# Attention with four score banks, transposes in place, value strips and tokens two pairs ahead, on one core

## The chip, the cores and the metric

One Trainium2 chip, one core of it. The metric is the device time of one execution in microseconds, on that core. The kernel before was run three times: median 1459.58 us, 1443.99 to 1460.77.

## What is computed

An audio tower of two layers on x of shape (16, 256, 256), all in float32. Cut to what the change touches:

```python
# first layer, tokens: 16 x 256 rows of 256 -> 16 x 128 tokens of 256
xb = x.reshape(16, 128, 2, 256)
t = einsum('btki,oik->bto', xb, conv_w) + conv_b + xb.mean(axis=2)
h = layernorm(t) * gamma + beta
# first layer, attention on layernorm(h): 16 heads of 16, the last 64 positions; h + attn @ Wo.T
# first layer, experts: top 2 of 16 with capacity, and a shared gated product
# second layer, attention on layernorm(h): 16 heads of 16, causal; h + attn @ w_out
# second layer, experts: top 3 of 64, gelu, 128 slots each
```

In both layers a head's scores are a 128 x 128 matrix per batch: softmax(mask + q k / 4), times v, divided by the sum of the exponentials. A router on the normalised result chooses experts and slots for each token.

## The kernel before

The sixteen batches are worked in eight pairs. One core runs five queues, each written out by hand in order, with semaphores between them: SyncE issues loads, TensorE multiplies and transposes, ScalarE takes exponentials and copies banks out, VectorE takes maxima, norms and the routing, GpSimd takes the square roots, the affine part of the first norm and the scatters of rows to expert slots. The stages follow each other: attention of the first layer, half of the shared product, sixteen gated experts, the rest of the shared product, attention of the second layer, 64 dense experts. The change touches the two attention stages and the start.

The eight accumulation banks of 512 columns: two for scores, two for transposed probabilities, one for the mix (all sixteen heads of both batches), two front banks for the jobs that bring a pair in (transposed x, convolution, transposed normed tokens, q, k, v) and one back bank for the jobs that bring it out (inverse sums turned, spread over the columns, output product, feed-forward input turned, router, counts). Jobs of front and back take their bank in a fixed order, and each waits until the job before it in that bank has been copied out (`front`, `front_job`, `back_job`, L758 and L1061).

Scores of a batch come in four quarters b of four heads. `scores` (L817) multiplies 32 rows of q, at row group b, with the keys of two heads, twice per quarter. A product in float32 is two instructions. `greatest` (L1443, VectorE) adds the mask, moves the scores to `probs` and takes the maxima, `exponentials` (L1188, ScalarE) works on them in place, `turn_probs` (L827) transposes four heads into a turn bank, `keep_turned` (L1197, ScalarE) copies it to `probsT`, and `values` (L842) multiplies it with `v_wide`, in which each head's sixteen columns stand in a block of 128 otherwise zero, so that all heads add into the full mix bank. `step` alternates scores of batch s with transposes and products of batch a, the one before it: body i of the loop `skewed_loop` runs `step` for (scores of (i, 0), rest of (i-1, 1)) and then for (scores of (i, 1), rest of (i, 0)).

Between them stand the other parts: `turn_x` (L767) and `conv` (L776) for pair i+1, whose result `mix_tokens` (L1405, L1410) adds to half of the sum of x that GpSimd made in `sum_x` (L616); `project_qk` (L795), `project_v` (L803), `spread_inverse` (L877), `project_out` (L887), `turn_ffn_in` (L896), `route` (L903), `count` (L913). VectorE's part is `pairs` at the end of its block: `front_a` to `front_d` for the norms (statistics L1378 and L1383, application L1390), `normalise` (L1459), `residual` (L1465), `choose` for the experts (L1487 to L1519) with `weigh` (L1534 to L1541), and `place` for the slots (L1550 to L1565), whose first operation takes the counts out of the back bank.

SyncE loads x of pair 1 after the weights; then it fills the slot arrays with zeros (L479, 15 transfers, 13 of them of 1 MB) and then loads x of pairs 2 to 7, each behind the transposes of the pair before.

## Time and profile before

| what | us |
|---|---|
| median of three runs (lowest, highest) | 1459.58 (1443.99, 1460.77) |
| profiled execution, its span | 1452.52, 1450.8 |
| TensorE busy, VectorE, ScalarE, GpSimd | 1314.3, 532.5, 565.7, 360.2 |
| mean granted clock of TensorE | 0.943 |
| first attention stage, window 43 to 345 | 302 |
| second attention stage, window 637 to 911 | 274 |

The profile is of one execution. Busy time is per engine, and a matmul's end is modelled. The granted clock is a share of 2.4 GHz; it has two levels, 1.00 and 0.50. The idle time of an engine comes with what ended it.

### The profile page before, as it was taken

How to read it: one execution, taken by the hardware profiler on the slowest of the kernel's cores; microseconds unless marked ns; L12 is line 12 of the kernel's file. 1: busy time of each engine (PE TensorE's matmuls, PEld its weight loads, DVE VectorE, ACT ScalarE, POOL GpSimd, SP SyncE). 2: the span in 40 equal slices, each digit the busy share in tenths (PEclk: the TensorE clock that was granted, in tenths of full speed). 3: DMA queues.
4: the chain of work that ended last, by engine and by line, in shares of the span. 5: the costliest groups of instructions: out<-in, count | busy, mean ns of one | idle time of the engine just before them, and what ended most of it. 6: DMA issues, size and time to landing. Idle time of an engine off the chain costs nothing.

```text
span 1450.8 us, 25791 instructions
## 1 busy us (share of the span) xinstructions
PE 1314.3 (91%) x7680; PEld 1105.3 (76%) x7680; DVE 532.5 (37%) x2676; ACT 565.7 (39%) x1960; POOL 360.2 (25%) x343
## 2 busy tenths in 40 slices
PE   5899999986888898879999998199999999999996
PEld 4677777773577677547778777199999999999995
DVE  4356566542234443332555555212211221222121
ACT  1666666651122222135666665033223223322331
POOL 3123333212035444400122222312112212221221
PEclk8899999987999899999999999599999999999998
DMA  9700000001156556351000000269999999999993
GB/s 332 295 16 30 29 29 29 15 12 40 63 121 144 130 113 144 69 191 68 16 24 9 8 7 7 84 221 304 306 312 310 303 305 317 304 304 309 315 297 78
DMA packets 148816, 218.04 MB, mean 150 GB/s; under 512 B 9604, under 2 KB 117094, under 8 KB 148737
## 3 DMA queue, kind: packets, MB, share of 16 engines
q1 hardware_dynamic: 129824, 197.18, 40.1%
q0 software_dynamic: 18944, 20.28, 8.3%
q8 instruction: 23, 0.38, 0.1%
q14 instruction: 25, 0.20, 0.0%
HBM read 178.51 MB, written 45.19 MB: 154 GB/s over the span
## 4 chain that ended last, share of the span: by engine, by line
PE 75%; issue 6%; DVE 6%; ACT 4%; DMA 4%; POOL 3%; POOLq 0%; DVEq 0%; SPq 0%; ACTq 0%
PE bank L1104 16%; PE bank L1117 15%; PE bank L817 9%; PE bank L842 6%; PE bank L827 4%; PE bank L795 4%; PE bank L998 3%; PE bank L1044 3%; ACT probs L1188 2%; PE bank L887 2%; DMA stream<-arena,slot_token 2%; PE bank L776 2%; PE bank L1119 2%; PE bank L1008 2%; PE bank L803 1%
## 5 line engine op out<-in xcount | busy, mean ns | idle before, releaser
L1343 ACT ACTIVATE dhidT<-bank,b1T 128x128 f32<-128x128 f32 x512 | 145.9, 368 | 335.9 <-PE bank L1104 335.9
L1104 PE MATMUL bank<-probsT,arena 128*128 128x128 f32 x2048 | 241.4, 277 | 0.1
L1104 PEld LDWEIGHTS bank<-probsT,arena 128*128 128x128 f32 x2048 | 236.0, 193 | 0.5 <-DVE probsT L1751 0.5
L1117 PE MATMUL bank<-arena,dhidT 128*128 128x256 f32 x1024 | 231.6, 379 | 0.0
L1117 PEld LDWEIGHTS bank<-arena,dhidT 128*128 128x128 f32 x1024 | 189.8, 190 | 23.2
L1188 ACT ACTIVATE probs<-probs,neg_max 128x128 f32<-128x128 f32 x512 | 197.9, 390 | 10.4 <-DVE neg_max L1443 10.1
L720 POOL DMA_INDIRECT stream<-probsT,slot_token x64 | 98.9, 1545 | 402.9 <-DMA stream<-probsT,slot_token 352.8
L1772 DVE TENSOR_SCALAR probsT<-bank,slot_gate 128x256 f32<-128x256 f32 x64 | 30.9, 483 | 384.9 <-PE bank L1119 378.9
L1443 DVE CUSTOM_DVE_ANT_0 probs<-bank,mask 128x128 f32<-128x128 f32 x512 | 117.4, 286 | 124.9 <-PE bank L817 122.3
L817 PE MATMUL bank<-kT,qT 32*128 32x256 f32 x512 | 146.9, 412 | 4.5 <-DVE neg_max L1443 2.1
L634 POOL DMA_INDIRECT rows<-ffn_in,scatter_i x80 | 79.8, 998 | 259.4 <-DVE scatter_i L1565 207.2
L842 PE MATMUL bank<-probsT,v_wide 128*128 128x128 f32 x1024 | 141.4, 285 | 1.5 <-ACT probsT L1197 1.3
L1197 ACT ACTIVATE probsT<-bank 128x512 f32<-128x512 f32 x128 | 75.2, 589 | 157.3 <-PE bank L827 117.4
L842 PEld LDWEIGHTS bank<-probsT,v_wide 128*128 128x128 f32 x1024 | 130.2, 199 | 2.2 <-ACT probsT L1197 2.1
L817 PEld LDWEIGHTS bank<-kT,qT 32*128 32x128 f32 x512 | 86.8, 191 | 39.0 <-issue 20.8
L1188 ACT ACTIVATION_READ_ACCUMULATOR probs<-probs,neg_max 128x1 f32 x512 | 97.1, 190 | 0.0
L691 POOL DMA_INDIRECT stream<-arena,slot_token x48 | 72.9, 1518 | 57.2 <-DVE arena L1714 45.3
L827 PEld LDWEIGHTS bank<-ident,probs 128*128 128x128 f32 x512 | 55.7, 145 | 41.1 <-issue 36.1
L827 PE MATMUL bank<-ident,probs 128*128 128x128 f32 x512 | 86.3, 293 | 0.0
L1056 PE MATMUL bank<-arena 128*128 128x256 f32 (+3 forms) x288 | 70.8, 394 | 13.2 <-DVE arena L1714 13.1
L1319 ACT ACTIVATE arena<-bank 128x320 f32<-128x320 f32 (+1 forms) x48 | 20.9, 436 | 152.5 <-PE bank L1044 116.1
L1056 PEld LDWEIGHTS bank<-arena 128*128 128x128 f32 (+3 forms) x288 | 48.4, 175 | 29.9 <-DVE arena L1714 17.5
(172 smaller groups left out, 1719.8 us busy)
## 6 DMA issues: line engine op xcount, KB each, us to landing
arena<-L_ffn_w SPq DMA_DIRECT2D x128, 1024.0 KB, 7.4
rows<-zeros SPq DMA_DIRECT2D x13, 1024.0 KB, 13.1
drows<-rows SPq DMA_DIRECT2D x64, 132.0 KB, 7.7
arena<-L_ffn_w_gate SPq DMA_DIRECT2D x16, 352.0 KB
arena<-L_ffn_w_up SPq DMA_DIRECT2D x16, 352.0 KB
early<-rows SPq DMA_DIRECT2D x16, 264.0 KB, 2.7
early<-x SPq DMA_DIRECT2D x8, 512.0 KB
arena<-L_ffn_w_down SPq DMA_DIRECT2D x16, 256.0 KB
```

Of the source, the lines that this page charges most:

```text
L634: g.indirect_dma_start(L.rows, bass.IndirectOffsetOnAxis(ap=scatter_i[:, k, t:t + 1], axis=0), ffn_in[:, t, :], None, bounds_check=L.E * L ...
L720: g.indirect_dma_start(stream, bass.IndirectOffsetOnAxis(ap=slot_token[:, u, 0:1], axis=0), dy[:, u % 2, :], None, bounds_check=N + NCT * ...
L817: last = pe.matmul(score_bank[b % 2][:, 2 * m * P:2 * (m + 1) * P], qT[row:row + 32, m, t, :], kT[row:row + 32, m, t, :, :], start=True, s ...
L827: last = pe.transpose(turn_bank[b % 2][:, j * P:(j + 1) * P], probs[:, t, head(b, j), :], ident[:, :])
L842: last = pe.matmul(mix_bank[:, col:col + P], v_wide[:, DC * t + m, own * P:(own + 1) * P], probsT[:, b, j * P:(j + 1) * P], start=b == 0 a ...
L1056: mm = pe.matmul(bank[6 + (NCT * u + s) % 2][0:m, 0:D], hidT[u][0:fm, j, r:r + m], down_w[u][0:fm, j, :], start=j == 0, stop=j == NFT - 1)
L1104: mm = pe.matmul(bank[2 + 2 * (u % 2) + half][:, jj * P:(jj + 1) * P], w1_sb[u][:, c, j * P:(j + 1) * P], drowsT[:, u % 2, c, :], start=c ...
L1117: pe.matmul(bank[6 + u % 2][:, 0:D], dhidT[:, u % 2, j, :], w2_sb[u][:, j, :], start=j == 0, stop=False)
L1188: last = act.activation(probs[:, t, hd, :], probs[:, t, hd, :], ACT.Exp, scale=-1.0, bias=neg_max[:, t, hd:hd + 1], accum_out=exp_sum[:, t ...
L1197: act.activation(probsT[:, b, :], turn_bank[b % 2][:, :], ACT.Copy).then_inc(L.turned, 1)
L1343: last_ = act.activation(dhidT[:, u % 2, j, :], bank[2 + 2 * (u % 2) + half][:, jj * P:(jj + 1) * P], ACT.Gelu, bias=b1T[:, j, bass.ds(e, 1)])
L1443: last = dve.tensor_tensor_reduce(probs[:, t, hd, :], score_bank[b % 2][:, j * P:(j + 1) * P], L.mask[:, :], -1.0, 3e38, ALU.add, ALU.min, ...
```

## The change

- Four score banks instead of two, and no turn banks. `scores` writes all sixteen heads of a batch in eight products, the four row groups in turn, with one signal at the end; it waits for all four copies of the batch before. `turn_probs` writes over the scores in their own bank.
- The copies of three quarters stay on ScalarE (`keep_turned`); the last is a copy on VectorE (`keep_last_turned`).
- `v_wide` becomes `v_pad`: two heads to a strip of 32 columns. `values` writes strip b of the mix bank, four strips in turn, a whole batch at a time.
- Tokens two pairs ahead: `turn_x` and `conv` of pair i+2 run in body i, pair 1 ahead of the loop. x of pair 1 is loaded before the router's inputs, x of pairs 2 and 3 behind the zero fills.
- The half sum of x goes into the diagonal of the convolution weights, once; `sum_x` goes.
- The order of all queues in `pairs` is new; each body finishes its own transposes. Job numbers of the banks come from two lists of the order.

```diff
-        score_bank, turn_bank, mix_bank = bank[0:2], bank[2:4], bank[4]
+        score_bank, mix_bank = bank[0:4], bank[4]
...
-        HALF = (P // HD) * (P + HD)
-        v_wide = sb("v_wide", [P, 2 * DC, HALF])
+        STRIP = 2 * HD
+        v_pad = sb("v_pad", [P, 2 * DC, (P // HD) * STRIP])
...
+            order = [(0, INVERSE)]
+            for i in range(1, PAIRS + 2):
+                for p, k in ((i - 2, COUNT), (i - 1, SPREAD), (i - 1, OUT), (i - 1, TURN_FFN), (i - 1, ROUTE), (i, INVERSE)):
+                    if 0 <= p < PAIRS:
+                        order += [(p, k)]
+            return {job: n for n, job in enumerate(order)}
...
-            load_x(1, False)
             sp.wait_ge(const_p, 3)
             fill_zeros()
-            with sp.Fori(2, PAIRS) as i:
+            for i in range(2, 4):
+                load_x(i, False)
+            with sp.Fori(4, PAIRS) as i:
...
+                wait(pe, L.turned, 6 * i + 3 * t)
+                wait(pe, L.turned_last, 2 * i + t)
                 for m in range(DC):
-                    last = pe.matmul(score_bank[b % 2][:, 2 * m * P:2 * (m + 1) * P], qT[row:row + 32, m, t, :],
-                                     kT[row:row + 32, m, t, :, :], start=True, stop=True)
+                    for b in range(SBANKS):
+                        row = 32 * b
+                        last = pe.matmul(score_bank[b][:, 2 * m * P:2 * (m + 1) * P], qT[row:row + 32, m, t, :],
+                                         kT[row:row + 32, m, t, :, :], start=True, stop=True)
...
-                n = 8 * i + 4 * t + b
-
-                wait(pe, L.exp_done, n + 1)
-                wait(pe, L.turned, n - 1)
+
+                wait(pe, L.exp_done, 8 * i + 4 * t + b + 1)
                 for j in range(HEADS_PER_BANK):
-                    last = pe.transpose(turn_bank[b % 2][:, j * P:(j + 1) * P], probs[:, t, head(b, j), :], ident[:, :])
+                    last = pe.transpose(score_bank[b][:, j * P:(j + 1) * P], probs[:, t, head(b, j), :], ident[:, :])
...
+                    m, r = divmod(j, 2)
                     col = (2 * m + t) * P
-                    last = pe.matmul(mix_bank[:, col:col + P], v_wide[:, DC * t + m, own * P:(own + 1) * P],
-                                     probsT[:, b, j * P:(j + 1) * P], start=b == 0 and j == 0,
-                                     stop=b == SBANKS - 1 and j % 2 == 1, skip_group_check=True)
+                    for b in range(SBANKS):
+                        own = 2 * b + r
+                        last = pe.matmul(mix_bank[b * STRIP:(b + 1) * STRIP, col:col + P],
+                                         v_pad[:, DC * t + m, own * STRIP:(own + 1) * STRIP], probsT[:, b, j * P:(j + 1) * P],
+                                         start=j == 0, stop=r == 1, skip_group_check=True)
...
+                    ahead = L is L0 and there(i + 2, PAIRS)
+                    if now:
+                        scores(L, i, 0)
                     if before_:
-                        turn_inverse(L, i - 1)
-                    if next_ and L is L0:
-                        turn_x(i + 1)
-                    if next_ and L is L1:
-                        turn_normed(L1, i + 1)
+                        values(L, i - 1, 1)
+                    if there(i - 2, PAIRS):
+                        count(L, i - 2)
                     if before_:
                         spread_inverse(L, i - 1)
-                    if next_ and L is L0:
-                        conv(i + 1)
-                    if next_ and L is L1:
-                        project_qk(L1, i + 1, 0)
-                        project_qk(L1, i + 1, 1)
+                    if now:
+                        project_v(L, i)
+                        turn_probs(L, i, 0, 0)
+                    if ahead:
+                        turn_x(i + 2)
+                    if now:
+                        turn_probs(L, i, 0, 1)
                     if before_:
                         project_out(L, i - 1)
                     if now:
-                        step(L, (i, 1), (i, 0), beside_second)
-                    else:
-                        beside_second(SBANKS - 1)
-                    if next_ and L is L0:
-                        turn_normed(L0, i + 1)
+                        turn_probs(L, i, 0, 2)
+                        turn_probs(L, i, 0, 3)
+                        scores(L, i, 1)
+                        values(L, i, 0)
+                    if next_:
+                        turn_normed(L, i + 1)
+                    if now:
+                        turn_probs(L, i, 1, 0)
+                    if ahead:
+                        conv(i + 2)
+                    if next_:
+                        project_qk(L, i + 1, 0)
+                    if now:
+                        turn_probs(L, i, 1, 1)
+                    if next_:
+                        project_qk(L, i + 1, 1)
+                    if now:
+                        turn_probs(L, i, 1, 2)
                     if before_:
+                        turn_ffn_in(L, i - 1)
                         route(L, i - 1)
-                    if next_ and L is L0:
-                        project_qk(L0, i + 1, 0)
-                        project_qk(L0, i + 1, 1)
-                    if next_:
-                        project_v(L, i + 1)
+                    if now:
+                        turn_probs(L, i, 1, 3)
+                        turn_inverse(L, i)
...
+                    ahead = L is L0 and there(i + 2, PAIRS)
+                    if now:
+                        exponentials(L, i, 0, 0)
+                    if there(i - 2, PAIRS) and L is L1:
+                        router_exp(L1, i - 2)
                     if before_:
                         keep_spread(L, i - 1)
                     if now:
-                        step(L, (i, 1), (i, 0), beside_second)
-                    else:
-                        beside_second(SBANKS - 1)
-                    if next_ and L is L0:
-                        keep_normedT(L0, i + 1)
+                        exponentials(L, i, 0, 1)
+                        keep_turned(L, i, 0, 0)
+                        keep_v(L, i)
+                        exponentials(L, i, 0, 2)
+                        keep_turned(L, i, 0, 1)
+                        exponentials(L, i, 0, 3)
+                        keep_turned(L, i, 0, 2)
+                    if ahead:
+                        keep_xT(i + 2)
+                    if now:
+                        exponentials(L, i, 1, 0)
+                    if next_:
+                        keep_normedT(L, i + 1)
+                    if now:
+                        exponentials(L, i, 1, 1)
+                        keep_turned(L, i, 1, 0)
+                        exponentials(L, i, 1, 2)
+                    if next_:
+                        keep_q(L, i + 1)
+                    if now:
+                        exponentials(L, i, 1, 3)
+                        keep_turned(L, i, 1, 1)
+                    if next_:
+                        keep_k(L, i + 1)
+                    if now:
+                        keep_turned(L, i, 1, 2)
+                    if before_:
+                        keep_ffn_inT(L, i - 1)
+                    if now:
+                        keep_inverse(L, i)
...
+            for k in range(2):
+                for c in range(DC):
+                    own = conv_wT[:, 2 * k + c, c * P:(c + 1) * P]
+                    last = dve.scalar_tensor_tensor(out=own, in0=ident[:, :], scalar=0.5, in1=own, op0=ALU.mult, op1=ALU.add)
+            last.then_inc(conv_ready, 1)
...
-                    dve.scalar_tensor_tensor(out=tok[:, t, :], in0=x_sum[:, t, :], scalar=0.5, in1=front_bank[b][:, 0:D],
-                                             op0=ALU.mult, op1=ALU.add).then_inc(L0.front_free[b], 1)
+                    dve.tensor_tensor(tok[:, t, :], front_bank[b][:, 0:D], conv_b[:, :], ALU.add).then_inc(L0.front_free[b], 1)
...
+            def keep_last_turned(L, i, t):
+
+                wait(dve, L.turn_full, 8 * i + 4 * t + SBANKS)
+                wait(dve, L.pv_done, 2 * i + t)
+                dve.tensor_copy(probsT[:, SBANKS - 1, :], score_bank[SBANKS - 1][:, :]).then_inc(L.turned_last, 1)
...
+                    ahead = L is L0 and there(i + 2, PAIRS)
                     if now:
-                        if before_:
-                            invert(L, i - 1, 1)
                         greatest(L, i, 0, 0)
                     if there(i - 2, PAIRS) and L is L1:
                         less_greatest(i - 2)
                     if now:
-                        greatest(L, i, 0, 1)
-                    if now and next_ and L is L1:
+                        for b in range(1, SBANKS):
+                            greatest(L, i, 0, b)
+                    if next_ and L is L0:
+                        front_c(i + 1)
+                    if next_ and L is L1:
                         front_a(L1, i + 1, False)
-                    if there(i - 2, PAIRS) and L is L1:
-                        weigh(L1, i - 2)
-                    if not now and there(i - 2, PAIRS):
-                        place(L, i - 2)
-                    if not now and before_:
-                        invert(L, i - 1, 1)
-                    if now:
-                        greatest(L, i, 0, 2)
-                        greatest(L, i, 0, 3)
-                    if next_ and L is L1:
-                        front_d(L1, i + 1)
-                    if now and there(i - 2, PAIRS):
+                    if there(i - 2, PAIRS):
+                        if L is L1:
+                            weigh(L1, i - 2)
                         place(L, i - 2)
                     if before_:
                         normalise(L, i - 1)
-                    if next_ and L is L0:
-                        front_a(L0, i + 1, False)
-                    if before_:
                         residual(L, i - 1)
+                        residual_stats(L, i - 1)
+                    if next_:
+                        front_d(L, i + 1)
                     if now:
+                        keep_last_turned(L, i, 0)
                         invert(L, i, 0)
-                        greatest(L, i, 1, 0)
-                    if before_:
-                        residual_stats(L, i - 1)
-                    if next_ and L is L0:
-                        front_b(i + 1)
-                    if now:
-                        greatest(L, i, 1, 1)
-                        greatest(L, i, 1, 2)
+                        for b in range(SBANKS):
+                            greatest(L, i, 1, b)
                     if before_:
                         expert_input(L, i - 1)
-                    if next_ and L is L0:
-                        front_c(i + 1)
+                    if ahead:
+                        front_a(L0, i + 2, False)
+                        front_b(i + 2)
                     if now:
-                        greatest(L, i, 1, 3)
-                    if next_ and L is L0:
-                        front_d(L0, i + 1)
+                        invert(L, i, 1)
+                        keep_last_turned(L, i, 1)
                     if before_:
                         choose(L, i - 1)
-                    if before_ and L is L0:
-                        weigh(L0, i - 1)
-
-                skewed_loop(dve, PAIRS, 2, body)
+                        if L is L0:
+                            weigh(L0, i - 1)
```

GpSimd's order in the first layer becomes: scale for the norm of i+1, scatter of i-2, scale for the feed-forward norm of i-1, addition of the input, scale and affine part of the tokens of i+2. `count` and `spread_inverse` keep their products; `spread_inverse` and `route` wait in addition for the copy of the job that feeds them.

## Rows read from the trace of the kernel before

**Rows 1.** Windows: the two attention stages, and one pair of each

```profile
core 0: us, PE busy (x) PEld busy (x) DVE busy (x) ACT busy (x) POOL busy (x), PEclk, DMA share, GB/s
43.00:345.00 302.00, 278.83 (x1600) 223.40 (x1598) 161.89 (x935) 174.33 (x633) 83.91 (x100) 0.95 0.13 47
188.80:225.90 37.10, 35.45 (x212) 28.66 (x211) 22.10 (x125) 22.97 (x84) 11.81 (x15) 1.00 0.08 29
...
637.00:911.00 274.00, 258.61 (x1468) 206.02 (x1468) 137.70 (x860) 170.56 (x647) 53.41 (x69) 0.94 0.11 40
750.40:781.90 31.50, 31.00 (x186) 24.79 (x187) 18.32 (x113) 21.02 (x82) 7.80 (x10) 1.00 0.05 19
```

**Rows 2.** TensorE timeline, one first-layer pair (start us, us, engine, line, operation, tiles, count)

```profile
188.74 3.72 PE L776 MATMUL bank<-conv_wT,early 128*128 128x256 f32 x16
...
211.15 1.89 PE L803 MATMUL bank<-wT,normedT 128*128 128x256 f32 x8
212.97 1.12 PE L817 MATMUL bank<-kT,qT 32*128 32x256 f32 x4
214.03 0.66 PE L827 MATMUL bank<-ident,probs 128*128 128x128 f32 x4
...
216.16 1.06 PE L842 MATMUL bank<-probsT,v_wide 128*128 128x128 f32 x8
...
224.76 1.12 PE L877 MATMUL bank<-exp_invT,own_rows 16*128 16x256 f32 x4
```

**Rows 3.** Groups by line, the same pair (busy us, mean ns, idle before, releaser)

```profile
L1188 ACT ACTIVATE probs<-probs,neg_max 128x128 f32<-128x128 f32 x32 | 12.4, 391 | 0.4 <-DVE neg_max L1443 0.3
...
L1443 DVE CUSTOM_DVE_ANT_0 probs<-bank,mask 128x128 f32<-128x128 f32 x32 | 7.3, 284 | 5.7 <-PE bank L817 5.7
...
L1197 ACT ACTIVATE probsT<-bank 128x512 f32<-128x512 f32 x8 | 4.7, 587 | 9.2 <-PE bank L827 9.2
...
L1170 ACT ACTIVATE kT<-bank,parity 128x512 f32<-128x512 f32 x2 | 1.3, 684 | 1.1 <-PE bank L795 1.1
```

**Rows 4.** VectorE timeline, the same pair

```profile
194.93 0.69 DVE L1465 TENSOR_TENSOR h<-h,bank 128x512 f32 x1
...
201.89 0.74 DVE L1378 BATCH_NORM_STATS2 stats<-h 128x6 f32 x2
...
207.75 0.19 DVE L1487 TENSOR_TENSOR logits<-bank,rb 128x32 f32<-128x32 f32 x1 [1.62 <-PE bank L903]
...
211.89 0.16 DVE L1541 TENSOR_TENSOR weight<-top_v,rsmall 128x4 f32<-128x4 f32 x1
...
222.41 0.19 DVE L1550 COPY count_sb<-bank 128x32 f32<-128x32 f32 x1 [0.52 <-PE bank L914]
...
224.23 0.15 DVE L1565 TENSOR_TENSOR scatter_i<-slotf,tmpf 128x4 int32<-128x4 f32 x1
```

**Rows 5.** TensorE timeline, first scores of the second layer

```profile
642.87 1.14 PE L817 MATMUL bank<-kT,qT 32*128 32x256 f32 x8
```

**Rows 6.** Timelines of the SyncE queue and of GpSimd, start of the kernel

```profile
55.90 58.04 SPq L407 DMA_DIRECT2D early<-x  x3
...
67.57 1.28 POOL L616 TENSOR_TENSOR early<-early 128x512 f32<-128x512 f32 x1 [10.67 <-DMA early<-x]
```

**Rows 7.** Windows: three stretches at the end of the first attention stage

```profile
290.00:300.00 10.00, 7.99 (x55) 6.18 (x53) 4.02 (x29) 7.77 (x32) 1.33 (x2) 0.94 0.01 2
300.00:310.00 10.00, 9.76 (x25) 6.57 (x26) 3.77 (x23) 2.13 (x9) 3.60 (x5) 0.50 0.11 41
310.00:345.00 35.00, 23.59 (x139) 19.43 (x138) 13.53 (x82) 13.49 (x40) 7.48 (x8) 0.74 0.04 12
```

**Rows 8.** TensorE timeline: first scores of pairs 1 and 7, and of pair 7

```profile
65.07 1.13 PE L817 MATMUL bank<-kT,qT 32*128 32x256 f32 x4
...
286.25 1.12 PE L817 MATMUL bank<-kT,qT 32*128 32x256 f32 x4
...
868.40 1.10 PE L817 MATMUL bank<-kT,qT 32*128 32x256 f32 x4 [0.32 <-issue]
```

273 lines of the change are left out of this document (128 added, 145 removed).

## Prediction

> **What bounds the kernel now.** I read the page's chain of waits first: three quarters of the span are TensorE, and its lines change with the stage, so the question is which stages the change touches. The windows answer it: first-layer attention from 43 to 345 us and second-layer attention from 637 to 911 us, 576 of 1450.8 us [rows 1]. The gated experts, the shared product and the dense experts between and behind them keep their code; I take them at their time. Then I took one pair of each layer. A first-layer pair lasts 37.1 us with TensorE busy 35.45 of it at granted clock 1.00; a second-layer pair lasts 31.5 us at clock 1.00. ScalarE and VectorE have 22 to 23 us of work per pair [rows 1]. TensorE's queue is the bound, and the other two run beside it because one batch's scores alternate with the preceding batch's transposes and products. The steady pace over whole stages is (286.25 - 65.07)/6 = 36.9 us, and (868.40 - 642.87)/7 = 32.2 us in the second layer, whose first pair is shorter [rows 5, 8].
>
> **The change part by part, TensorE's work.** Scores of one quarter of a batch, four instructions, take 212.97 to 214.03 = 1.06 us; a batch has four, 4.2 us [rows 2]. Now all four row groups follow each other. The old trace has that in small: where the pipeline is empty two quarters stand back to back, and eight instructions take the 1.14 us that four take elsewhere [rows 5, 2]. Their pace, 1.14 less the tail of about 0.25, is 0.11 us each; sixteen make 1.8 us. Bounds: 4.2 us (no overlap) and 16 x 0.22/4 = 0.9 us (four at once, at the pace of the 16 instructions of 256 columns in 3.56 us). I take 1.8, the nearest row. Products with the values: a quarter is eight instructions in about 0.9 us, a batch 3.6 [rows 2]. As strips of 32 output partitions no row shows them; bounds 3.6 and 0.9 us, I take 1.9, since the score row halves too. The rest of a pair (transposes 0.5 a quarter, convolution 3.6, the query and key product 3.6, value and output products 1.8 each, spread 1.0) stays. TensorE's own work falls from 35.4 to about 27 us in the first layer.
>
> By the Trainium skill ("TensorE: Matmul & The Clock Gate", Packing small matmuls), four row tiles gave 3.07 times and three column tiles 2.38 times; estimated from that page, scores would be 1.4 and products 1.5 us, 0.8 us a batch below my sum. The trace agrees that row groups overlap.
>
> **What takes its place.** The transposes now overwrite the score banks, so scores of a batch wait until all four banks of the preceding one are copied out (three by ScalarE, one by VectorE). Batches no longer overlap, and the pace is that of a chain from copy to copy. I follow it through a first-layer pair in the new order of the queues; zero is the end of the last copy before it.
>
> First half. VectorE has the choice of experts queued behind that copy and ahead of the next maxima: 207.75 to 212.05 = 4.3 us [rows 4], and 0.4 because the exponential it needs is behind a copy on ScalarE: 4.7. Scores (1.8) are hidden under it, so neither packing nor banks helps here. Four maxima quarters at 0.85 (thirty-two heads, 7.3 us busy, [rows 3]): 8.1. Statistics of the next pair 0.74 + 0.25 + 0.1 [rows 4]: 9.2. Only then comes the copy of the counts, the first operation of the slot calculation, 0.2: 9.4. It matters because there is one back bank: the spread of the inverses may not begin before the counts have left it. Behind the spread TensorE holds the value product and the first transpose, and ScalarE holds the copy of the spread ahead of the second quarter's exponentials. So: spread 1.05, value product 1.8, transpose and its landing 0.8 [rows 2]: 13.1. ScalarE copies it and the values, 0.5 each: 14.1. The second early transpose of x waits for that bank: 0.6, next transpose 0.5, output product 1.8 and 0.25 to VectorE: 17.2. Residual 0.7, statistics 1.1, normalisation 0.7 [rows 4], then the new last copy 0.7 (512 columns from a bank, as the residual): 20.4. TensorE idles about 5 us ahead of the spread.
>
> Second half, from 0 again. Scores 1.8, products 1.9, transpose of the normed tokens 0.5, first transpose by 5.0 (its exponentials end at 4.5: scores 1.8, landing 0.25, maxima 0.9, exponentials 1.55, from 12.4 us for 32 heads [rows 3]), convolution two pairs ahead 3.6, query product 1.8, landing: 10.65. ScalarE, which holds that copy ahead of the last exponentials, goes on: 0.6, exponentials 1.55, copy 0.5, keys 1.25, copy 0.5, feed-forward input 0.6 [rows 3]: 15.65. Routing 0.85, last transpose and landing 0.8, last copy 0.7: 18.1. The pair: 38.5 us at full clock, against 37.1.
>
> Second layer: choice without weights 3.5, maxima and one small operation 3.5, statistics 1.1, weights 0.6, counts 0.3: 9.0; spread, value product, transpose 3.65; two copies 1.0; exponentials, copy, exponentials 3.6; last transpose and copy 1.5: 18.75. Second half, now bound by ScalarE because there is no convolution: 16.15. Together 34.9 at full clock against 31.5.
>
> **The clock.** Stretches in which TensorE was busy 8.0 of 10 us were followed by 10 us at 0.50, which is 1.2 GHz, and the 35 us with 23.6 us busy had 0.74 [rows 7], while the full pair had 1.00 [rows 1]. The new pair is busy 27 of 38.5 us, 70%, with a gap ahead of the spread in each. I take 0.87 as mean clock, between 0.74 and 1.00, so work in the chain grows by 15%: 17.5 us of the first-layer chain is TensorE (5.75 in the first half, 11.75 in the second), +2.6, pair 41.1; 7.0 us in the second layer, +1.1, pair 36.0.
>
> The same page (HAM oscillation) says that pauses between bursts send the array back to its half rate: a rule against this change. The trace agrees: [rows 7] show the drop behind a thinner stretch. By it alone, with every pair dipping, the time is that of the clock rival below.
>
> **The start.** The tokens of pair 2 are now transposed in pair 0, between its first and second probability transpose, but their load stays behind the zero fills in SyncE's queue: issued at 55.90, landed at 67.57, where GpSimd's sum was waiting for it [rows 6]. TensorE, strictly in order, waits there. From 67.5: two transposes 1.2, probability transpose 0.8, copy 0.5, exponentials 1.55, transpose 0.8, last copy 0.7: 73. Second half without routing 18: first scores of pair 1 at 91, before 65.07 [rows 8]. The loss is about 26 us; with the load early enough it would be some 2 us.
>
> **Smaller parts, taken at nothing.** The halved sum of x goes into the convolution weights (four small operations once, ahead of a VectorE fill that shrinks by three quarters): saves GpSimd 1.3 and VectorE 0.8 us a pair, both off the chain. Moving one load of x ahead of the router loads delays these by 2 to 3 us; the normalised first pair hides that. One more pair unrolled, no cost. GpSimd's scatters start after the slots, at 11 us, and land before the feed-forward input is due in the second half; if not, that is 1 to 3 us a pair. The stages' tails stay as they are: the last copies no longer straddle pairs, but the slots come later; between -6 and +3 us each.
>
> **The sum.** First layer: 91, pair 1 at 33.5 (no choice, no slots yet), five at 41.1: first scores of pair 7 at 330, against 286.25: +44. Second layer from its first scores: 28, 29.5, five at 36.0: 237.5 against 868.40 - 642.87 = 225.5: +12. The profiled execution took 1452.52 us (span 1450.8 and 1.7 around it): 1452.5 + 56 = 1508. It is 7 us below the median of the three runs shown, 1459.58, within their spread.
>
> **Rivals.**
> 1. Clock near 0.70 in both stages. For: the 0.74 of [rows 7]. Against: TensorE works through most of the second half. Pairs 38.5 + 17.5 x 0.43 = 46 and 37.9: ten pairs add 34 us, 1542.
> 2. Full packing and full clock: scores 0.9, products 1.0. Pairs 36.8 and 34.2, start still late: first layer +19, second +2, 1474. For: the row of eight. Against: the gap per pair.
> 3. The other side: VectorE's small operations do not stand in the chain, neither the choice ahead of the maxima nor the counts ahead of the spread (the choice over while the last exponentials run). Pairs 30.6 and 30.4; with the late start -12 and -15: 1426. Against it stands the order of VectorE's queue and the single back bank; for it, that VectorE is busy only 22 of 37 us. It decides once a first-layer pair lasts less than about 31 us, or 33 with a start that is not late.
> 4. The packing does not come: scores 4.2, products 3.6, about 4.1 and 3.5 us a pair more: 1554. [Rows 5] speak against it for scores; if only the strips fail, 1524, inside my range.
>
> **Chances.** Forecast 0.52 (own range 1480 to 1530), rival 1 0.12, rival 2 0.20, rival 3 0.12, rival 4 0.04. A measurement of this kernel can tell about 2%, 29 us. Slower by over that: most of the forecast, rivals 1 and 4: 0.63; within: the rest of the forecast and rival 2: 0.25; faster: 0.12. The range reaches from 1455, most of rival 2, to 1542.
>
> **What would show it.** Right: a TensorE gap of some 20 us that a load of x ends, between 45 and 68 us; first-layer pairs 39 to 43 us apart; sixteen score instructions in about 2 us; the spread starting within 0.1 us of the copy of the counts; maxima starting where the choice ends, not where the scores end; PEclk under 0.95 in both stages. Wrong: pairs under 36 us, ScalarE waiting for the spread less than 1 us, or no wait on x.

## The result, and the profile after

The changed kernel takes 1521.52 us (median of 4 runs, 1518.83 to 1525.41) against 1458.17 us for the kernel before: a ratio of 1.045, interval 1.041 to 1.049. It is slower. The profiled execution took 1520.47 us, with a span of 1518.7 against 1450.8 before. Line numbers from here on are those of the changed kernel: scores L862, probability transposes L870, values L886, spread L908, output product L918, maxima L1484, last copy L1493, counts copy L1597. In an experiment's rows some lie a few lines further on.

The windows come first. A pair has two halves, each from the first scores of a batch to those of the next. The first row is one pair's length of the first layer, from second scores to second scores; the second row is the first half in it, the third the second half behind it. The fourth is a second-layer pair, the last the thin part of a first half. They answer to [rows 1].

```profile
core 0: us, PE busy (x) PEld busy (x) DVE busy (x) ACT busy (x) POOL busy (x), PEclk, DMA share, GB/s
183.25:224.20 40.95, 28.75 (x211) 22.21 (x211) 20.74 (x126) 21.28 (x82) 10.75 (x13) 0.79 0.08 26
201.15:224.20 23.05, 15.01 (x97) 11.12 (x97) 12.52 (x78) 10.73 (x42) 6.02 (x8) 0.67 0.14 46
224.20:242.10 17.90, 13.74 (x114) 11.09 (x115) 8.22 (x48) 10.54 (x41) 4.73 (x5) 0.95 0.00 0
818.84:856.32 37.48, 26.57 (x186) 19.82 (x187) 19.22 (x117) 19.75 (x80) 7.85 (x10) 0.73 0.03 9
205.30:216.50 11.20, 6.24 (x19) 4.53 (x17) 6.62 (x49) 3.78 (x17) 3.83 (x5) 0.50 0.07 24
```

TensorE is busy for less time, 28.75 us instead of 35.45 in a pair, yet the pair lasts 40.95 us instead of 37.10. No engine is full any more: the pace is that of a chain. Now TensorE's timeline of that pair (start us, us, engine, line, operation, tiles, count, idle before and releaser):

```profile
201.15 2.14 PE L862 MATMUL bank<-kT,qT 32*128 32x256 f32 x16 [0.16 <-issue]
203.22 1.94 PE L886 MATMUL bank<-probsT,v_pad 128*32 128x128 f32 x32
...
210.32 2.07 PE L908 MATMUL bank<-exp_invT,own_rows 16*128 16x256 f32 x4 [4.96 <-DVE count_sb L1597]
212.32 3.78 PE L845 MATMUL bank<-wT,normedT 128*128 128x256 f32 x8
...
224.20 1.15 PE L862 MATMUL bank<-kT,qT 32*128 32x256 f32 x16 [2.06 <-DVE probsT L1493]
225.27 1.08 PE L886 MATMUL bank<-probsT,v_pad 128*32 128x128 f32 x32
```

The packing works. At full clock sixteen score products take 1.15 us, where four quarters of 1.06 took 4.2 [rows 2]; thirty-two strips take 1.08 us, where values took 3.6. But at 201.15 they run at half rate, then TensorE stands still for 4.96 us, and the spread and the value product behind it take 2.07 and 3.78 us instead of 1.12 and 1.89: 2.84 us from the clock alone. VectorE's timeline says what TensorE waited for:

```profile
199.54 0.69 DVE L1493 COPY probsT<-bank 128x512 f32<-128x512 f32 x1 [4.02 <-PE bank L870]
200.15 0.18 DVE L1534 TENSOR_TENSOR logits<-bank,rb 128x32 f32<-128x32 f32 x1
...
204.76 0.16 DVE L1588 TENSOR_TENSOR weight<-top_v,rsmall 128x4 f32<-128x4 f32 x1
205.68 0.29 DVE L1484 CUSTOM_DVE_ANT_0 probs<-bank,mask 128x128 f32<-128x128 f32 x1 [0.76 <-DVE weight L1588]
...
209.07 0.75 DVE L1423 BATCH_NORM_STATS2 stats<-h 128x6 f32 x2
209.92 0.25 DVE L1428 BATCH_NORM_AGGREGATE moments<-stats 128x2 f32<-128x6 f32 x2
210.08 0.18 DVE L1597 COPY count_sb<-bank 128x32 f32<-128x32 f32 x1
```

The choice of experts runs from 200.15 to 204.92, the maxima start behind it, 0.76 us later, although the scores were there at 203.3, then come the statistics, and only at 210.08 do the counts leave the back bank. The spread starts at 210.32. At the start, TensorE's wait for the tokens of pair 2, and the DMA queue of SyncE that explains it:

```profile
64.89 1.97 PE L806 MATMUL bank<-ident,early 128*128 128x128 f32 x8 [22.91 <-DMA early<-x]
```

```profile
19.14 34.70 SPq L526 DMA_DIRECT2D rows<-zeros  x15
...
55.22 1.27 SPq L452 DMA_DIRECT2D early<-x  x1
```

The page's groups show the sums over the whole kernel (busy us, mean ns, idle before and releaser): 52.4 us of waiting for the counts, and 119.7 us in which ScalarE's exponentials wait for maxima. The last row is that group in the window 183.25 to 224.20 alone: 8.2 us, against 0.3 in the pair before [rows 3].

```profile
L1228 ACT ACTIVATE probs<-probs,neg_max 128x128 f32<-128x128 f32 x512 | 198.2, 392 | 119.7 <-DVE neg_max L1484 119.7
...
L862 PE MATMUL bank<-kT,qT 32*128 32x256 f32 x512 | 53.3, 545 | 24.9 <-DVE probsT L1493 19.6
L908 PE MATMUL bank<-exp_invT,own_rows 16*128 16x256 f32 x64 | 31.0, 632 | 52.4 <-DVE count_sb L1597 52.4
...
L1228 ACT ACTIVATE probs<-probs,neg_max 128x128 f32<-128x128 f32 x32 | 12.4, 393 | 8.2 <-DVE neg_max L1484 8.2
```

Where the 67.9 us of span came from, by the first scores of each pair. Pair 1 starts at 87.18 instead of 65.07: +22.1. From there to pair 7 (321.39): +13.0. From pair 7 to the first scores of the second layer (688.26): 366.9 against 356.6 us, +10.3. Second layer to its pair 7 (931.39): 243.1 against 225.5, +17.6. The rest: 587.3 against 582.4, +4.9.

Two of these stretches hold both changed and unchanged code, so they are cut once more, before and after. The first row of each fence is the sixteen gated experts with the work between them, the second is the second layer from the first scores of pair 7 to the first product of the dense experts, the third is the dense experts to the end:

```profile
389.21:600.73 211.52, 184.92 (x949) 153.96 (x949) 88.49 (x221) 50.95 (x108) 92.04 (x59) 0.93 0.53 119
868.40:942.78 74.38, 40.87 (x244) 31.90 (x244) 31.43 (x176) 23.30 (x86) 19.77 (x22) 0.78 0.14 44
942.78:1450.80 508.02, 493.48 (x3324) 460.44 (x3324) 99.26 (x511) 147.14 (x513) 98.87 (x64) 0.98 0.89 285
```

```profile
425.08:646.32 221.24, 192.45 (x948) 159.28 (x949) 93.06 (x221) 50.96 (x108) 93.43 (x60) 0.89 0.51 114
931.39:1011.16 79.77, 37.11 (x235) 26.23 (x234) 33.01 (x182) 19.52 (x80) 19.80 (x22) 0.59 0.13 41
1011.16:1518.70 507.54, 493.18 (x3324) 460.14 (x3324) 99.27 (x511) 147.14 (x513) 98.87 (x64) 0.98 0.89 285
```

So 9.7 of the 10.3 us are lost in the gated experts, whose code did not change, and the +4.9 at the end is the tail of the second attention stage, +5.4, while the dense experts take the same time as before.

### The profile page after: what moved, and what is told of

It is laid out like the page before. It is cut to its first block, busy times and chain, and to the rows that moved or that the text cites. A ratio compares the mean times of both kernels' runs of the same rounds, so it can differ in the third digit from the quotient of the medians.

```text
span 1518.7 us, 25449 instructions
## 1 busy us (share of the span) xinstructions
PE 1216.9 (80%) x7680; PEld 1006.7 (66%) x7680; DVE 535.7 (35%) x2696; ACT 539.9 (36%) x1928; POOL 351.4 (23%) x335
## 4 chain that ended last, share of the span: by engine, by line
PE 58%; DVE 12%; ACT 11%; issue 8%; DMA 5%; SPq 3%; POOL 2%; DVEq 0%; POOLq 0%; ACTq 0%
PE bank L1143 15%; PE bank L1156 14%; ACT probs L1228 7%; PE bank L1083 4%; PE bank L1037 3%; PE bank L845 3%; DVE probs L1484 3%; SPq L526 2%; PE bank L870 2%; PE bank L862 2%; PE bank L1158 2%; PE bank L908 2%; DMA stream<-arena,slot_token 2%; ACT probsT L1237 2%; PE bank L935 1%
## 5 line engine op out<-in xcount | busy, mean ns | idle before, releaser
L1228 ACT ACTIVATE probs<-probs,neg_max 128x128 f32<-128x128 f32 x512 | 198.2, 392 | 119.7 <-DVE neg_max L1484 119.7
L1156 PEld LDWEIGHTS bank<-arena,dhidT 128*128 128x128 f32 x1024 | 189.8, 190 | 23.2
L1484 DVE CUSTOM_DVE_ANT_0 probs<-bank,mask 128x128 f32<-128x128 f32 x512 | 111.2, 286 | 42.5 <-PE bank L862 37.6
L870 PE MATMUL bank<-ident,probs 128*128 128x128 f32 x512 | 92.4, 315 | 40.3 <-ACT probs L1228 40.1
L870 PEld LDWEIGHTS bank<-ident,probs 128*128 128x128 f32 x512 | 71.7, 166 | 62.3 <-ACT probs L1228 55.4
L656 POOL TENSOR_SCALAR var_eps<-moments 128x2 f32<-128x2 f32 x40 | 9.7, 242 | 374.3 <-DVE moments L1428 374.3
L1237 ACT ACTIVATE probsT<-bank 128x512 f32<-128x512 f32 x96 | 56.0, 585 | 50.5 <-PE bank L870 50.5
L862 PE MATMUL bank<-kT,qT 32*128 32x256 f32 x512 | 53.3, 545 | 24.9 <-DVE probsT L1493 19.6
L908 PE MATMUL bank<-exp_invT,own_rows 16*128 16x256 f32 x64 | 31.0, 632 | 52.4 <-DVE count_sb L1597 52.4
L1095 PEld LDWEIGHTS bank<-arena 128*128 128x128 f32 (+3 forms) x288 | 49.7, 180 | 34.2 <-DVE arena L1752 20.4
L1083 PE MATMUL bank<-rows_high,gate_up_high 128*128 128x320 f32 (+1 forms) x192 | 66.4, 346 | 1.4 <-DVE gate_up_low L99 1.0
```

The source lines that it names most:

```text
L862: last = pe.matmul(score_bank[b][:, 2 * m * P:2 * (m + 1) * P], qT[row:row + 32, m, t, :], kT[row:row + 32, m, t, :, :], start=True, stop= ...
L870: last = pe.transpose(score_bank[b][:, j * P:(j + 1) * P], probs[:, t, head(b, j), :], ident[:, :])
L1083: mm = pe.matmul(dst[0:m, 0:C0], wp, xp[:, c, :], start=c == 0 and n == 0, stop=c == DC - 1 and n == 2)
L1095: mm = pe.matmul(bank[6 + (NCT * u + s) % 2][0:m, 0:D], hidT[u][0:fm, j, r:r + m], down_w[u][0:fm, j, :], start=j == 0, stop=j == NFT - 1)
L1156: pe.matmul(bank[6 + u % 2][:, 0:D], dhidT[:, u % 2, j, :], w2_sb[u][:, j, :], start=j == 0, stop=False)
L1228: last = act.activation(probs[:, t, hd, :], probs[:, t, hd, :], ACT.Exp, scale=-1.0, bias=neg_max[:, t, hd:hd + 1], accum_out=exp_sum[:, t ...
```

## The experiments

Every kernel was timed in three rounds. Ratios are to the kernel before, which stood at 1455.6 to 1463.0 us in these runs; the changed kernel's is 1.0451 [1.0409, 1.0493]. The first four were run together, each with one edit to the changed kernel.

**Early x.** The load of pair 2 goes behind the fifth zero fill:

```diff
+ if fill is fill0 and at == 4 * P * FILL:
+     load_x(2, False)
...
- for i in range(2, 4):
-     load_x(i, False)
+ load_x(3, False)
```

> Edit: x of pair 2 is loaded behind the fifth zero fill instead of behind all of them. Chain theory: the 22.9 us gap of TensorE ahead of the second early transposes shrinks to what the queue of fills leaves, 0 to 8 us, so the kernel takes 1500 to 1507 us, 15 to 21 less than the changed one (1521.5). Rival (the gap only moves, since the transfers fill the DMA queues anyway and pair 3's load or the scatter's wait for the fills comes late instead): 1516 to 1522 us.

Measured: 1503.1 us, ratio 1.0311 [1.0244, 1.0378]. The wait of 22.91 us is now 0.47, and pair 1 starts at 65.38:

```profile
42.39 1.11 PE L807 MATMUL bank<-ident,early 128*128 128x128 f32 x4 [0.47 <-DMA early<-x]
...
65.38 1.15 PE L863 MATMUL bank<-kT,qT 32*128 32x256 f32 x16 [1.34 <-ACT probsT L1238]
```

So the late load cost some 18 us of time, as expected. The pairs behind it stayed at 39.4 to 42.8 us.

**Counts.** The copy of the counts moves from the head of the slot calculation to behind the first quarter of the maxima:

```diff
  greatest(L, i, 0, 0)
+ take_counts(L, i - 2)
  for b in range(1, SBANKS):
      greatest(L, i, 0, b)
```

> Edit: VectorE takes the counts out of the back bank behind the first quarter's maxima, not behind the fourth and the statistics. Chain theory: the spread starts 3.5 us earlier in 12 pairs, and 5 us of gap ahead of it shrink to 1 to 1.5; the first half is then bound by VectorE's path and ends 2 to 3 us earlier, and less of it runs at half clock. 30 to 45 us less than the changed kernel: 1476 to 1492. Rival (the first half is bound by maxima, slots, output product and normalisation on VectorE anyway): 0 to 10 us less, 1511 to 1521. Rival (everything is clock): the granted clock of a pair stays at 0.73 to 0.79 and less than 10 us come back.

Measured: 1479.35 us, ratio 1.0131 [1.006, 1.0203]. The place of this single copy of 0.18 us is worth 42 us, in the expected range. TensorE's wait ahead of the spread falls from 4.96 to 1.43 us. The full pairs of the first layer fall to between 35.0 and 37.7 us (38.6 to 41.2 before the edit), those of the second to between 33.8 and 37.3 (37.0 to 38.1). The granted clock hardly moves, so the rival that everything is clock is out:

```profile
198.54 2.07 PE L908 MATMUL bank<-exp_invT,own_rows 16*128 16x256 f32 x4 [1.43 <-DVE count_sb L1595]
```

```profile
192.95:230.37 37.42, 28.70 (x210) 22.06 (x211) 20.61 (x125) 21.27 (x83) 10.75 (x13) 0.82 0.09 28
790.30:824.14 33.84, 26.76 (x186) 19.80 (x187) 19.19 (x117) 19.75 (x80) 7.84 (x10) 0.75 0.03 10
```

**Busy TensorE.** The value products of each second batch are issued five times, to raise the clock:

```diff
- for j in range(HEADS_PER_BANK):
+ for j in (list(range(HEADS_PER_BANK)) * (5 if t == 1 else 1)):
```

> Edit: the values product of each pair's second batch is run five times instead of once, with the same result, so that TensorE works through most of the gap of 5 us ahead of the spread; it adds 4.3 us of TensorE's work per pair at full clock, 8.6 at half. Theory that the thin stretch brings the clock down and that this costs about 3 us in the first half of each pair: clock of a pair rises above 0.9, the spread and value product run at full speed, pairs are 1 to 3 us shorter in spite of more work; 1480 to 1510 us. Rival (the clock's fall has another cause, or is no cost): the pairs keep their 41.0 and 37.5 us or grow by up to 4; 1521 to 1580.

Measured: 1512.26 us, ratio 1.0383 [1.0311, 1.0454], which overlaps the changed kernel's interval. The clock did rise:

```profile
202.02:240.33 38.31, 30.25 (x338) 24.64 (x339) 20.76 (x125) 21.27 (x83) 10.76 (x13) 0.90 0.08 28
811.81:849.14 37.33, 28.71 (x314) 22.41 (x315) 19.17 (x117) 19.65 (x80) 7.85 (x10) 0.82 0.03 9
```

From 0.79 to 0.90 and from 0.73 to 0.82. The pair shown is 2.6 us shorter than that of the changed kernel, the other full pairs of the layer 0.8 to 3.0; from pair 1 to pair 7 the first layer takes 228.1 us against 234.2, the second 240.4 against 243.1. The time lies just above the range of the theory and below that of the rival. Added work raised the clock and pairs got shorter in spite of it, so the low clock is a real cost. This filler stands partly in the chain that it is to speed up and bought back 9 us at most, within overlapping intervals; filler outside that chain was not tried.

**All copies on ScalarE.** The last of the four copies of a batch goes back to ScalarE:

```diff
- dve.tensor_copy(probsT[:, SBANKS - 1, :], score_bank[SBANKS - 1][:, :]).then_inc(L.turned_last, 1)
+ act.activation(probsT[:, SBANKS - 1, :], score_bank[SBANKS - 1][:, :], ACT.Copy).then_inc(L.turned_last, 1)
```

> Edit: the last of the four copies of a batch back on ScalarE (behind the third in the first half, behind the feed-forward input in the second). Chain theory: in the second half ScalarE is free when the last transpose lands, the copy ends at the same time but VectorE no longer stands behind it, so the choice of experts starts 1.2 to 1.5 us earlier; in the first half the copy comes 0.5 us earlier. Pairs 1 to 2 us shorter: 1497 to 1512. Rival (ScalarE is the bound of the pair and its 0.6 us a batch count): pairs 1.2 us longer, 1530 to 1545.

Measured: 1497.95 us, ratio 1.0261 [1.0192, 1.033], at the better end of the theory's range. Handing a copy to VectorE cost 24 us, through what it queues behind there. In the changed kernel's first half the last transposes, from 221.49, are out by 222.2, but the copy waits for the normalisation:

```profile
222.81 0.73 DVE L1435 TENSOR_SCALAR normed<-h,moments,rstd 128x256 f32 x2
223.46 0.68 DVE L1493 COPY probsT<-bank 128x512 f32<-128x512 f32 x1
```

In the second half it stands ahead of the logits (200.15 above), for which TensorE's inverse transposes wait. On ScalarE the copy runs beside both: first halves of 21.0 to 21.8 us instead of 21.8 to 23.3.

**Scores twice.** A price for the scores in the chain:

```diff
- for m in range(DC):
+ for m in [0, 1, 0, 1]:
```

> The 16 score products of every batch are issued twice (the second time over the same banks, same values), 32 batches, 1.15 us each at full clock and 2.1 at half. My theory, scores of a first half are hidden behind the choice of experts on VectorE, so only those of second halves count: 16 batches times 1.1 us, at most +16 to +20 us, 1535 to 1545 us; the first halves stay at 23.0 and 21.1 us in the profile. Rival, scores stand in the chain of both halves: +37 to +50 us, 1558 to 1570 us, both halves longer. Third possibility, TensorE's clock rises by the added work and pays for it: no change or faster.

Measured: 1551.7 us, ratio 1.0622 [1.0554, 1.069]: 30 us more than the changed kernel, between my two theories. In the first layer I was right: first halves stay at 21.8 to 23.4 us, since 3.62 us of scores are still hidden behind the choice, and four of the five full pairs grow by 1.4 to 2.6 us. I missed the clock: in the second half, where one set took 1.15 us at full rate, two take 3.15.

```profile
209.00 3.62 PE L862 MATMUL bank<-kT,qT 32*128 32x256 f32 x32 [0.42 <-issue]
...
232.07 3.15 PE L862 MATMUL bank<-kT,qT 32*128 32x256 f32 x32 [2.14 <-DVE probsT L1493]
```

In the second layer the choice is shorter (3.45 us against 4.77), and both halves grow: four of the five full pairs take 40.6 to 41.9 us against 37.0 to 37.5.

**A later choice.** The choice goes behind the maxima, the counts behind the output product, the slots to the middle of the second half, and GpSimd's scale for the feed-forward norm ahead of the scatter:

```diff
- ((i - 2, COUNT), (i - 1, SPREAD), (i - 1, OUT), (i - 1, TURN_FFN), ...
+ ((i - 1, SPREAD), (i - 1, OUT), (i - 2, COUNT), (i - 1, TURN_FFN), ...
...
  for b in range(1, SBANKS):
      greatest(L, i, 0, b)
  front_c(i + 1)
+ choose_rest(L, i - 2)
...
  greatest(L, i, 1, 1)
+ place(L, i - 2)
```

> Only the logits and what frees the back bank stay at the end of a pair; the choice of the preceding pair's experts runs behind the four maxima of the next first batch, and the counts go through the back bank after the output product instead of before the spread. x of pair 2 is still late. My theory, the choice ahead of the maxima and the counts ahead of the spread together open the gap in the first half: it falls from 23.0 to 16.5 to 18.5 us, pairs 34 to 37 us, 1445 to 1485 us. Rival, the low clock and the serial order of the banks make the gap, not VectorE's small operations: first half above 21 us, 1505 to 1520 us.

Measured: 1548.74 us, ratio 1.0611 [1.0541, 1.068]. Half of my theory held: the first half is 17.3 us instead of 23, and with that the choice and the counts together are shown as what opened the gap. The time is 27 us worse instead of better, outside both ranges. The second half is 25.8 instead of 17.9, and these two rows of VectorE's and GpSimd's timelines show why:

```profile
232.22 0.73 DVE L1437 TENSOR_SCALAR ffn_in<-h,moments,rstd 128x256 f32 x2 [5.62 <-DMA rows<-ffn_in,scatter_i]
```

```profile
225.79 1.09 POOL L676 DMA_INDIRECT rows<-ffn_in,scatter_i  x1 [5.73 <-DVE scatter_i L1624]
```

The scatters of the preceding pair now start at 225.79, so the next feed-forward input may not overwrite their source before 232.22, and the convolution's bias waits behind it on VectorE. This is the price that the prediction had named for late scatters (1 to 3 us a pair); here the wait alone is 5.6, and the half is 7.9 longer.

**Convolution later,** behind the query and key products:

```diff
  turn_probs(L, i, 1, 0)
- conv(i + 2)
  project_qk(L, i + 1, 0)
...
  turn_probs(L, i, 1, 2)
+ conv(i + 2)
```

> The convolution of two pairs ahead runs behind the query and key products instead of before them (first layer only, second layer unchanged). My theory, in the second half the convolution delays the copy of the queries, behind which ScalarE holds the last exponentials; the second half falls from 17.9 to 16.0 to 17.0 us in seven pairs: 1507 to 1515 us. Rival, the later convolution makes VectorE late with its bias and statistics, which stand ahead of the last copy: second half 18 us or more, 1520 to 1530 us.

Measured: 1531.96 us, ratio 1.0485 [1.0414, 1.0556]; the rival, 2 us above its range. The second halves of the full first-layer pairs but the last take 18.9 to 19.5 us instead of 17.7 to 17.9. The statistics of the early tokens come late, and the last copy is queued behind them on VectorE:

```profile
247.12 0.42 DVE L1449 TENSOR_TENSOR early<-bank,conv_b 128x256 f32<-128x256 f32 x1 [2.44 <-PE bank L818]
...
249.94 0.73 DVE L1435 TENSOR_SCALAR early<-early,moments,rstd 128x256 f32<-128x256 f32 x2 [1.20 <-POOL rstd L658]
...
250.75 0.63 DVE L1493 COPY probsT<-bank 128x512 f32<-128x512 f32 x1
```

**Three together**: early x, counts, all copies on ScalarE.

> Early load of x of pair 2, counts taken behind the first quarter of maxima, and the last copy back on ScalarE, all at once. Alone they gave 18, 42 and 24 us. If each shortens another piece of the chain: 1436 to 1450 us, level with or ahead of the kernel before at 1458. If the counts and the copy share one gap: 1455 to 1470 us.

Measured: 1430.72 us, ratio 0.9797 [0.9735, 0.9859]. It is faster than the kernel before, by 1.4 to 2.7%, and 91 us below the changed one, more than the 84 of the three edits alone and 5 us better than the expected range. So they shorten different pieces; why together they give 7 us more was not tried.

**Three, with the choice behind the maxima** and the slots early enough:

```diff
- ((i - 2, COUNT), (i - 1, SPREAD), (i - 1, OUT), ...
+ ((i - 1, SPREAD), (i - 2, COUNT), (i - 1, OUT), ...
...
+ choose_rest(L, i - 2)
  normalise(L, i - 1)
+ take_counts(L, i - 2)
+ place(L, i - 2)
  residual(L, i - 1)
```

> The three edits of the kernel at 1430.7 us (early x, last copy on ScalarE, counts out of the spread's way), with the choice of experts moved behind the maxima and the counts in the back bank between spread and output product, slots calculated before the residual, so that the scatters start some 5 us before the feed-forward input is due. My theory: the failure of the previous version with a later choice was the wait of the feed-forward input on the scatters, which is gone here, and the choice ahead of the maxima still costs 2 to 3 us a pair: pairs of 30.5 to 32 us, 1395 to 1420 us. Rival, the slots now stand ahead of the residual and lengthen the first half by what the choice saves, or the scatters are late again: 1425 to 1450 us.

Measured: 1439.55 us, ratio 0.9879 [0.9814, 0.9945]; the rival's range, but by another way than it said. The first half fell to 14.8 us from 16.8, the second rose to 19.3 from 17.0. The convolution, 3.62 us in the kernel of three edits, takes 5.31, which is 1.7 of these 2.3 us:

```profile
182.99 5.31 PE L819 MATMUL bank<-conv_wT,early 128*128 128x256 f32 x16
```

The windows of the two halves, first of the kernel of three edits, then of this one, show the mean clock of the pair unchanged at 0.90, but the slow stretches in other places:

```profile
163.85:180.67 16.82, 13.46 (x97) 10.01 (x97) 11.08 (x75) 10.28 (x42) 4.94 (x6) 0.80 0.17 55
180.67:197.62 16.95, 13.36 (x114) 11.12 (x115) 8.39 (x49) 11.99 (x44) 5.79 (x7) 1.00 0.02 9
```

```profile
163.04:177.84 14.80, 11.68 (x97) 8.89 (x98) 10.69 (x72) 10.28 (x42) 1.83 (x3) 0.89 0.11 35
177.84:197.14 19.30, 15.31 (x115) 12.38 (x115) 8.83 (x52) 12.10 (x44) 8.78 (x11) 0.91 0.08 28
```

The stretch at half clock has not gone; here it lies on the longest product of the pair (granted clock 0.68 over these 5.31 us), where in the kernel of three edits it lay on scores, values and the value product of the first half.

**Three, with the values of the second batch issued twice.**

> The kernel at 1430.7 us with the value products of every second batch issued twice, so that TensorE is busy 1.1 to 1.9 us more in each first half. If TensorE's clock still costs what it cost in the changed kernel, the clock of the pairs rises from 0.90 and 0.80 to 0.93 and 0.88 and the time falls to 1420 to 1428 us. If the work is only added to the chain ahead of the spread: 1435 to 1448 us.

Measured: 1433.22 us, ratio 0.9813 [0.9742, 0.9883]; no difference from the kernel without, and between the two expected ranges. In the profiles the clock from pair 1 to pair 7 is 0.92 instead of 0.90 in the first layer, which takes 196.2 us instead of 200.0, and 0.82 instead of 0.84 in the second, 233.3 instead of 226.0. With the gap mostly closed, this filling buys nothing on the whole.

**Three, with the router early.** The feed-forward transposes go ahead of the query product, the router product behind the second probability transpose, their copy and exponential ahead of the last copies:

```diff
  conv(i + 2)
+ turn_ffn_in(L, i - 1)
  project_qk(L, i + 1, 0)
  turn_probs(L, i, 1, 1)
+ route(L, i - 1)
  project_qk(L, i + 1, 1)
  turn_probs(L, i, 1, 2)
- turn_ffn_in(L, i - 1)
- route(L, i - 1)
```

> The kernel at 1430.7 us with the feed-forward transposes ahead of the query product, the router product behind the second probability transpose, and its copy and exponential ahead of the last copies on ScalarE, in both layers; so the choice of experts runs beside the last exponentials instead of ahead of the next maxima, and TensorE's wait of 1.9 us on the feed-forward copy falls away. My theory, these two are still in the chain: 2 to 2.5 us of the first half and 1 to 1.5 of the second, pairs 30.5 to 32 us at the same clock, 1390 to 1412 us. Rival, the clock takes the saving back, as it took it in the version with the choice behind the maxima (first half shorter, convolution at half clock): pairs 33 to 34.5 us, 1422 to 1440 us.

Measured: 1388.62 us (1387.23 to 1396.44), ratio 0.9548 [0.9501, 0.9595]. It is the fastest of all, 4.5% below the kernel before, and just below the expected range. Its windows, a first-layer pair with its halves, and one of the second layer:

```profile
156.59:187.45 30.86, 25.04 (x210) 20.26 (x210) 19.37 (x123) 22.36 (x85) 10.75 (x13) 0.94 0.10 35
156.59:171.68 15.09, 11.87 (x97) 9.16 (x97) 10.26 (x70) 10.14 (x41) 4.79 (x6) 0.89 0.17 61
171.68:187.45 15.77, 13.17 (x114) 11.10 (x114) 9.12 (x54) 12.22 (x45) 5.95 (x8) 1.00 0.02 9
714.37:745.64 31.27, 22.45 (x187) 17.34 (x187) 17.64 (x112) 20.74 (x82) 7.86 (x10) 0.89 0.03 11
```

The choice now ends 2.4 us behind the start of the next scores instead of 3.7, TensorE's wait of 1.9 us on the feed-forward copy is gone, and TensorE is granted 0.94 over this pair. The five full pairs take 29.6 to 32.5 us in the first layer and 29.0 to 33.4 in the second.

**The same, with the last copy on VectorE again,** in the second half between the logits and the rest of the choice:

> The fastest kernel so far (1388.6 us: early x, counts behind the first quarter of maxima, router early, all copies on ScalarE) with the last of the four copies of each batch back on VectorE; in the second half it stands between the logits and the rest of the choice. It asks whether that part of the change is bad in itself or only in its place. My theory: the copy costs what stands ahead of it (statistics and normalisation in the first half, about 1 us) and what it pushes behind it (the choice, 0.7 us): 1 to 2 us a pair, 1400 to 1415 us. Rival, it runs beside ScalarE's third copy and costs nothing or gains 0.5 us a half: 1375 to 1392 us.

Measured: 1416.52 us, ratio 0.973 [0.97, 0.9761]; 28 us slower, just above the range of my theory. The first halves of the full pairs take 15.4 to 18.7 us instead of 13.7 to 16.8, where the copy is again behind the normalisation; in the second the choice ends 2.9 us behind the start of the next scores instead of 2.4; and the clock of one pair (161.76 to 196.78) was 0.85. That part of the change is not worth keeping in this order either.

## Why the prediction was right, and where it was not

The sum was 1508 against 1521.5; the sign, the mechanism and the largest pieces held. That the sum came so near is in part luck: the first layer up to its pair 7 was forecast 44 us longer and was 35, and everything behind it was forecast 12 us longer and was 33.

- **The start.** Forecast: x waits behind the zero fills, pair 1 at 91. It was at 87.18, a loss of 22 instead of 26 us of span, and the early load shows that 18 us of time hang on it. TensorE went on at 64.9 instead of 67.5, and the second half took 15.3 instead of 18; the work between took 1.5 us more than was summed.
- **The choice ahead of the maxima, the counts ahead of the spread.** A gap of about 5 us was forecast; the row says 4.96. The counts kernel shows the counts as a cause: 42 us for one small copy moved. Moving the choice as well brought the first half to 17.3 us; on top of the three edits a later choice shortened the first half by 2.0 us and the pair by nothing. That batches no longer overlap, because the transposes share the score banks, is read from the waits; no run gave the old banks back.
- **A first-layer pair.** Forecast 41.1, measured 40.95 (the five lie between 38.6 and 41.2), but two errors cancel. The clock was taken as 0.87 throughout; it was 0.67 in the first half and 0.95 in the second. With 5.75 us of TensorE in the first half's chain, 0.67 makes 20.4 into 23.2 (measured 23.05). The packing was undersized: 1.8 and 1.9 us were taken, 1.15 and 1.08 measured, which saves the second half 1.5 us.
- **A second-layer pair.** Forecast 36.0, measured 37.5 (the five lie between 37.0 and 38.1): the first half is at clock 0.64 over the 21.2 us of its length. Here the two errors do not cancel, and the stage up to its pair 7 lost 17.6 us instead of 12.
- **The untouched stages.** This step failed: "I take them at their time." The dense experts kept theirs, 508 us at clock 0.98 in both kernels, but the gated experts took 221.24 us instead of 211.52, at clock 0.89 instead of 0.93. Each profile is of one execution, but all thirteen other kernels profiled here took longer for this stretch than the kernel before: 214.3 us (clock 0.91, router early) to 223.4 (0.87, all copies on ScalarE). What sets the clock there, in code that no edit touched, stays open; it was not tried.
- **The tails.** They were put at between -6 and +3 us each and at nothing in the sum. The first stage's tail kept its time (59.7 us from pair 7's first scores to the shared product, 60.1 before). The second's took 79.77 us instead of 74.38, at clock 0.59 instead of 0.78.
- **Rival 1** (clock near 0.70) was right on the clock, 0.79 and 0.73, and too high on the time, because the loss sits in half of the pair. **Rival 2** (full packing) was right on the packing, 1.15 and 1.08 us, and wrong on all else: what was saved on TensorE is hidden behind VectorE in the first half. **Rival 3** (VectorE's small operations out of the chain, pairs of 30.6 and 30.4) was not what the change did. The version with the router early comes near it: 30.86 and 31.27 in the pairs shown. **Rival 4** is excluded by the score and value rows.

The Trainium skill ("TensorE: Matmul & The Clock Gate", Packing small matmuls) gives 3.07 times for four row tiles and 2.38 for three column tiles, both at 512 columns. Here four row groups at 256 columns went from 4.2 to 1.15 us, 3.7 times, and four strips at 128 columns from 3.6 to 1.08 us, 3.3 times. So the prediction's estimates from that page, 1.4 and 1.5 us, were nearer than its own 1.8 and 1.9, and the measurement lies beyond both. The Trainium skill says on the same page (HAM oscillation) that a wait between bursts of products throttles TensorE again, so that the next burst starts slow. The trace agrees: the granted clock is 0.50 over the 11.2 us around the gap.

## What to carry to other kernels

When packing takes work off a full engine, draw the chain of hand-overs that remains before counting the saving: here the engine was busy 6.7 us less in a pair and the pair grew by 3.9, in the main since one bank shared by several small results tied TensorE to VectorE's queue. Then look for the small operations that stand ahead of others' releases: one copy of 0.18 us moved was worth 42 us, and the feed-forward transposes and router product moved up another 42. Take the clock per stretch, not per stage, because here the saving left a gap, and 2.84 us of a pair were paid back at half rate behind it.

## What had not been expected of the hardware

- Strips of 32 output partitions ran thirty-two products of 128 columns in 1.08 us, against 1.06 us for eight full ones [rows 2].
- The stretch at half clock can move. When the first half became shorter by 2 us, the convolution behind it took 5.31 instead of 3.62 us, and the pair gained nothing.
- An unchanged stage that begins 44 us behind the first attention stage ran at another granted clock (0.89 instead of 0.93 over the gated experts) and took 9.7 us longer; one that begins behind the second, the dense experts, did not (0.98 in both).
- Adding work raised the clock of a first-layer pair from 0.79 to 0.90, yet the time fell by less than 1%.
